# A fused attention and expert kernel: how the first batch's weights are signalled, loaded and split

## What is computed

```python
xn = _layernorm(x, axis=-1)
x = x + attention(xn, Wq, bq, Wk, bk, Wv, bv, Wo, bo) + experts(xn, ...)

# attention, 16 heads of 16
q, k = elu(xn @ Wq + bq) + 1, elu(xn @ Wk + bk) + 1
v = xn @ Wv + bv
kv = einsum('bkhd,bkhm->bhdm', k, v)
out = einsum('bqhd,bhdm->bqhm', q, kv)
out = out / maximum(einsum('bqhd,bkhd->bqh', q, k), 1e-6)[..., None]
return out @ Wo + bo

# experts: a shared swiglu, and the two best of four experts in the better of two groups
shared = swiglu(flat @ w_in.T) @ w_out.T
h = swiglu(flat @ w1.T)
routed = sum over e of (h * w_se[:, e:e + 1]) @ w2[e].T
return shared + routed
```

## Time and profile before

| | us |
|---|---|
| median of 3 runs | 922.63 (922.33 to 922.94) |
| the profiled execution | 922.05 |
| its span in the trace | 920.2 |
| TensorE busy | 903.5 (98%) |
| VectorE, ScalarE, GpSimd busy | 694.1, 367.3, 403.9 |
| mean granted TensorE clock | 0.996 |

### The profile page before, as it was taken

The page is one execution under the profiler, slowest core; times in us unless marked ns, Lnnn a source line. Parts: engine busy times, 40 slices in busy tenths (PEclk is TensorE's granted clock), DMA queues, the critical chain, the costliest instruction groups (busy, mean ns, idle before and its releaser), DMA issues. The chain is left out here.

```text
span 920.2 us, 22781 instructions
## 1 busy us (share of the span) xinstructions
PE 903.5 (98%) x6982; PEld 815.6 (89%) x6983; DVE 694.1 (75%) x1816; ACT 367.3 (40%) x605; POOL 403.9 (44%) x486
## 2 busy tenths in 40 slices
PE   8999999999999999999999999999999999999996
PEld 7798988889898989888898989898888999999996
DVE  6878777787868687777878696877676777777773
ACT  5654544353545445443525454453432222222220
POOL 3654342443425243424434243434242666555554
PEclk9999999999999999999999999999999999999999
DMA  6432413132322324141323223241156888888870
GB/s 216 136 116 70 125 51 120 69 103 90 93 100 93 116 69 125 46 125 69 103 80 103 91 92 126 69 125 47 59 204 144 145 143 143 148 137 135 137 128 1
DMA packets 141992, 98.63 MB, mean 107 GB/s; under 512 B 53136, under 2 KB 133008, under 8 KB 141968
## 3 DMA queue, kind: packets, MB, share of 16 engines
q1 hardware_dynamic: 103584, 62.50, 23.7%
q0 software_dynamic: 15920, 25.32, 12.5%
q10 hardware_dynamic: 22464, 10.51, 4.8%
HBM read 53.29 MB, written 46.43 MB: 108 GB/s over the span
## 5 line engine op out<-in xcount | busy, mean ns | idle before, releaser
L350 PE MATMUL bank<-wexp_hi,xnT_hi 128*128 (+1 forms) x560 | 188.1, 336 | 1.5 <-DVE xnT_lo L1149 1.1
L352 PE MATMUL bank<-wexp_hi,xnT_lo 128*128 (+1 forms) x560 | 185.7, 332 | 0.0
L351 PE MATMUL bank<-wexp_lo,xnT_hi 128*128 (+1 forms) x560 | 185.7, 332 | 0.0
L1227 POOL TENSOR_TENSOR h_lo<-gated,h_hi 128x256 fp32r<-128x256 f32 x128 | 98.7, 792 | 141.2 <-ACT h_hi L709 141.2
L350 PEld LDWEIGHTS bank<-wexp_hi,xnT_hi 128*128 128x128 f32 x560 | 106.3, 190 | 15.1 <-issue 4.6
L352 PEld LDWEIGHTS bank<-wexp_hi,xnT_lo 128*128 128x128 f32 x560 | 106.4, 190 | 10.3
L351 PEld LDWEIGHTS bank<-wexp_lo,xnT_hi 128*128 128x128 f32 x560 | 106.4, 190 | 9.5
L350 PE MATMUL bank<-xnT_hi,win_hi 128*128 128x512 f32 x256 | 102.1, 399 | 0.0
L351 PE MATMUL bank<-xnT_lo,win_hi 128*128 128x512 f32 x256 | 100.4, 392 | 0.0
L352 PE MATMUL bank<-xnT_hi,win_lo 128*128 128x512 f32 x256 | 99.6, 389 | 0.0
L1251 POOL TENSOR_TENSOR res<-res,bo_t 128x256 f32<-128x256 f32 x64 | 49.2, 801 | 112.3 <-DMA res<-x 112.3
(11 more groups left out here) (198 smaller groups left out, 2377.4 us busy)
## 6 DMA issues: line engine op xcount, KB each, us to landing
res<-x SPq DMA_DIRECT2D x16, 512.0 KB, 3.6
out<-res SPq DMA_DIRECT2D x16, 512.0 KB, 2.8
xt<-x SPq DMA_DIRECT2D x15, 512.0 KB, 3.4
xn_d<-xt SPq DMA_DIRECT2D x15, 512.0 KB, 4.9
xt<-xn_d SPq DMA_DIRECT2D x60, 128.0 KB, 2.7
xt<-h_d SPq DMA_DIRECT2D x76, 64.0 KB
xt<-h_d ACTq DMA_DIRECT2D x76, 64.0 KB
kb<-h_d SPq DMA_DIRECT2D x76, 64.0 KB
```

The lines of the kernel that those rows point to most:

```text
L350: e.matmul(to, w_hi, m_hi_, start=first_, stop=False, skip_group_check=free)
L351: e.matmul(to, w_hi, m_lo_, start=False, stop=False, skip_group_check=free)
L352: return e.matmul(to, w_lo, m_hi_, start=False, stop=last_, skip_group_check=free)
L1227: ins = pool.tensor_tensor(h_lo[:, j, cols], gated[:, j % 2, cols], h_hi[:, j, cols].bitcast(f32), ALU.subtract)
```

## The change

`kv_w_ld` becomes three semaphores, and ScalarE waits for each just ahead of its high part. `w_split` counts one more step, because W_k and router are split apart. The identity is loaded by itself; the rest of `stay`, and all loads of SP behind it, are issued after a wait for W_k, with the rest of `stay` behind W_q and the biases. VectorE makes W_k's low part ahead of the normalise, and W_v's ahead of the transposed x's. The five copies of constants move from ahead of the batch to after the statistics of batch 1, and the waits for them (`const_set`) move back on ScalarE and TensorE. On ScalarE the high part of w1's second half moves ahead of the exponential of the logits; on GpSimd the root of batch 1 moves behind the low part of w1's second half.

```diff
--- before.py
+++ after.py
@@ -187,14 +187,18 @@
         bank = [ctx.enter_context(nc.psum_tensor(f"bank{i}", [P, 512], f32)) for i in range(8)]
 
 
-        kv_w_ld = sem("kv_w_ld")
+        k_w_ld = sem("k_w_ld")
+        rt_w_ld = sem("rt_w_ld")
+        v_w_ld = sem("v_w_ld")
         q_w_ld = sem("q_w_ld")
         in_w_ld = sem("in_w_ld")
         out_w_ld = sem("out_w_ld")
         w1_ld = [sem(f"w1_ld{n}") for n in range(2)]
         x_ld = sem("x_ld")
         x0_ld = [sem(f"x0_ld{t}") for t in range(TB)]
+        ident_ld = sem("ident_ld")
         stay_ld = sem("stay_ld")
+        b_ld = sem("b_ld")
         c_ld = sem("c_ld")
         warm_set = sem("warm_set")
         r_ld = sem("r_ld")
@@ -365,10 +369,12 @@
             def loads(done, pairs, stage):
                 for to, of in [(buf, of) for buf, of, _, _ in stage] + pairs:
                     sp.dma_start(to, of).then_inc(done, 16)
-            loads(kv_w_ld, [], stage_kv[0:1])
-            sp.dma_start(stay[:, :], c_stay).then_inc(stay_ld, 16)
+            loads(k_w_ld, [], stage_kv[0:1])
+            sp.dma_start(ident, c_stay[:, 0:P]).then_inc(ident_ld, 16)
+            sp.wait_ge(k_w_ld, 16)
             loads(q_w_ld, [], stage_q)
-            loads(c_ld, [(bkl[:, :], b_kl), (bq[:, :], b_q)], [])
+            loads(b_ld, [(bkl[:, :], b_kl), (bq[:, :], b_q)], [])
+            sp.dma_start(stay[:, P:], c_stay[:, P:]).then_inc(stay_ld, 16)
             loads(in_w_ld, [], stage_in)
             loads(c_ld, [(round_f, c_round)], [])
             sp.wait_ge(xn_rdy, TB)
@@ -454,7 +460,7 @@
         def _(pe):
             def first_transposes():
 
-                pe.wait_ge(stay_ld, 16)
+                pe.wait_ge(ident_ld, 16)
                 for t in range(TB):
                     pe.wait_ge(xn_rdy, t + 1)
                     for c in range(DC):
@@ -501,7 +507,7 @@
                                  wk_hi[:, c, 0:KL], wk_lo[:, c, 0:KL], c == 0, c == DC - 1)
                     mm.then_inc(k_done, 1)
                     if first_row(b) and t == 0:
-                        pe.wait_ge(w_split, 2)
+                        pe.wait_ge(w_split, 3)
                     if t == 2:
                         pe.wait_ge(kb_rdy, TB * b + 1)
                     for c in range(DC):
@@ -511,7 +517,7 @@
                         mm.then_inc(v_done, 1)
 
                 if first_row(b):
-                    pe.wait_ge(w_split, 3)
+                    pe.wait_ge(w_split, 4)
                 for o in range(DC):
                     if o == 1:
                         wait(pe, base_rdy, DC * b - 1)
@@ -521,7 +527,6 @@
                     mm.then_inc(q_done, 1)
                 if first_row(b):
                     pe.wait_ge(ffn_split, 1)
-                    pe.wait_ge(const_set, 1)
                 wait(pe, base_rdy, DC * b)
                 pe.wait_ge(v_rdy, 2 * b + 1)
                 hidden(0, (6, 7))
@@ -545,6 +550,8 @@
                 pe.wait_ge(eq_rdy, DC * (b + 1))
                 routed(0, (3, 4))
 
+                if first_row(b):
+                    pe.wait_ge(const_set, 1)
                 pe.wait_ge(oh_rdy, b + 1)
                 W = NSLOT
                 pe.matmul(bank[5][:, 256:256 + TB * W], triones[:, 0, :], oh[:, :, :].rearrange("p t c -> p (t c)"),
@@ -629,7 +636,7 @@
 
             warm_up(WARM)
             first_transposes()
-            pe.wait_ge(w_split, 1)
+            pe.wait_ge(w_split, 2)
             rounds(pe, batch, B)
 
 
@@ -714,8 +721,7 @@
 
             def batch(b, last):
                 if first_row(b):
-                    act.wait_ge(w_split, 3)
-                    act.wait_ge(const_set, 1)
+                    act.wait_ge(w_split, 4)
                 for i in range(2):
                     act.wait_ge(v_done, 2 * b + i + 1)
                     wait(act, acc_done, b)
@@ -731,11 +737,13 @@
                     if first_row(b) and i == 0:
                         act.wait_ge(w1_ld[0], 16)
                         high_parts(stage_w1[0:1])
+                if first_row(b):
+                    act.wait_ge(w1_ld[1], 16)
+                    high_parts(stage_w1[1:2])
                 act.wait_ge(lg_rdy, b + 1)
                 act.activation(ex[:, :, :], lg[:, :, :], ACT.Exp).then_inc(ex_rdy, 1)
                 if first_row(b):
-                    act.wait_ge(w1_ld[1], 16)
-                    high_parts(stage_w1[1:2])
+                    act.wait_ge(const_set, 1)
                 for o in range(DC):
                     act.wait_ge(q_done, DC * b + o + 1)
                     act.wait_ge(phik_rdy, 2 * b + o + 1)
@@ -774,10 +782,11 @@
 
             for t in (1, 3):
                 act.dma_start(xt[:, t, :], x[0, t * P:(t + 1) * P, :]).then_inc(x0_ld[t], 16)
-            for buf, of, _, _ in stage_kv[1:3]:
-                act.dma_start(buf, of).then_inc(kv_w_ld, 16)
-            act.wait_ge(kv_w_ld, 16 * 3)
-            high_parts(stage_kv)
+            for (buf, of, _, _), done in zip(stage_kv[1:3], (rt_w_ld, v_w_ld)):
+                act.dma_start(buf, of).then_inc(done, 16)
+            for n, done in enumerate((k_w_ld, rt_w_ld, v_w_ld)):
+                act.wait_ge(done, 16)
+                high_parts(stage_kv[n:n + 1])
             first_high()
             act.wait_ge(q_w_ld, 16)
             high_parts(stage_q)
@@ -975,6 +984,16 @@
                 dve.wait_ge(rsil_rdy, TB * b + t + 1)
                 dve.tensor_tensor(hs[t], hs[t], bank[up_bank][:, :], ALU.mult).then_inc(rg_rdy, 1)
 
+            def constants_in():
+                dve.wait_ge(c_ld, 16)
+                dve.wait_ge(stay_ld, 16)
+                dve.tensor_scalar(nbq[:, :], bq[:, :], -1.0, None, ALU.mult)
+                dve.tensor_copy(triones[:, 0, :], tri_f)
+                dve.tensor_copy(spread[:, :, :], spread_f)
+                dve.tensor_copy(run[:, :], slot_row)
+                dve.tensor_copy(tok[:, :], tok0).then_inc(const_set, 1)
+                dve.wait_ge(const_set, 1)
+
             def batch(b, last):
                 start(LN_LINKS + PER * b)
 
@@ -999,6 +1018,7 @@
                     k_in(t)
                     if first_row(b) and t == 2:
                         stats_in(1)
+                        constants_in()
                     if first_row(b) and t == 3:
                         norm_out(1, True)
                     if t == 1 and not first_row(b) and not last:
@@ -1153,21 +1173,14 @@
             dve.memset(kvT[:, :, :], 0.0)
             start(0)
             norm(0)
+            low_parts(stage_kv[0:1], 0)
             first_normalise()
-            low_parts(stage_kv[0:2], 0)
+            low_parts(stage_kv[1:2], 1)
+            low_parts(stage_kv[2:3], 2)
             first_low()
-            low_parts(stage_kv[2:3], 2)
             low_parts(stage_q, len(stage_kv))
-            dve.wait_ge(c_ld, 16 * 3)
-            dve.wait_ge(kv_w_ld, 16 * 3)
-            dve.wait_ge(stay_ld, 16)
-            dve.tensor_scalar(nbq[:, :], bq[:, :], -1.0, None, ALU.mult)
-            dve.tensor_copy(triones[:, 0, :], tri_f)
-            dve.tensor_copy(spread[:, :, :], spread_f)
-            dve.tensor_copy(run[:, :], slot_row)
-            dve.tensor_copy(tok[:, :], tok0).then_inc(const_set, 1)
-            dve.wait_ge(const_set, 1)
-            dve.wait_ge(w_split, 3)
+            dve.wait_ge(b_ld, 16 * 2)
+            dve.wait_ge(w_split, 4)
             rounds(dve, batch, B)
 
             def add(t, g, n, to):
@@ -1300,8 +1313,7 @@
             for n in range(2):
                 pool.wait_ge(w_round, first + len(stage_in) + n + 1)
                 low_part(stage_w1[n][0], stage_w1[n][2], stage_w1[n][3], w1_split)
-                if n == 0:
-                    reciprocal_root(1)
+            reciprocal_root(1)
             in_low(2)
             in_low(3)
             pool.wait_ge(w_round, first + len(stage_in) + len(stage_w1) + 1)
```

## The result

The changed kernel took 924.85 us in the median (922.59 to 925.96), the kernel before 922.42 (920.65 to 923.66) on the same chips. The ratio is 1.0025 (95% interval 1.0018 to 1.0032): slower by 2.3 us (2.4 between the medians), just over the 0.2% that can be told from no change. The forecast was 922.1, a difference too small to be told. The profiled execution of after took 924.81 us, its span 923.0, 2.8 us over the span of before.

What follows compares the result with a forecast made beforehand. TensorE, busy 98% of the span, was taken as the bound, so only an earlier L588, its last first-batch wait, would count. Terms summed to -0.5 us there: 922.05 to 921.55, median 0.58 above, 922.1; range 920.7 to 923.3.

Steps and rivals of the forecast that it cites:

- The SP queue: Loads held behind the wait for W_k: W_in's landing unchanged, likely within -0.6 to +1.0 us; x at 14.2 us.
- sum for a clock that stays up: VectorE's K bias of row block 3 if TensorE's clock stays up: x last, 14.3 + 1.4 + 1.4 = 17.1 us, -1.0.
- The copies: Constants' copies on VectorE between batch 1's statistics and row block 3's K bias: cost 1.4 us, bounds 0.67 to 2.3.
- The first K matmul: TensorE's start: earlier W_k rounding and identity bring the first K matmul to 9.86 us from 10.61, -0.75.
- The moved root: GpSimd's root moved behind w1's low parts: contention costs VectorE +0.5 us at phiq, between -0.3 and +1.5.
- GpSimd's chain: GpSimd's low parts up to W_in: two gaps lost, 0.9 us, so the end at 28.3 plus any W_in delay.
- ScalarE behind phiq: ScalarE's early w1 cast frees it before gate(0) ends: -0.7 us between phiq and gate(1), gate(1) -0.5 in all.
- TensorE still gets there first: At L588 TensorE, 0.2 us later, still arrives before qn_hi, having waited 1.2 us, so L588 moves by -0.5.
- The sum: All terms together: phiq +0.2 us, L588 -0.5, profiled execution 921.55, median 922.1.
- Both signs: Prediction wrong if phiq starts before 28.7 or after 30.2 us, or TensorE waits between 14 and 27 us.
- Rival B: The load queue's hole makes W_in 2.5 us late: phiq +1.5, L588 +0.8, 923.4 us; chance 0.12.

Runs made afterwards that it cites:

- d1: The changed kernel repeated without any edit, against the kernel before: +1.7 us, ratio 1.0018 (1.0009 to 1.0026).
- a1: The changed kernel without SyncE's wait for W_k: +0.9 us against the kernel before, ratio 1.0010 (1.0001 to 1.0018).
- b3: The kernel before with only the five copies of constants moved behind batch 1's statistics: +0.8 us, ratio 1.0008 (0.9999 to 1.0017).
- c1: a6 with the copies of constants ahead of batch 1's statistics and the root back between w1's low parts: +0.4 us against before, ratio 1.0002.
- e1: c1 with the copies of constants at their old place, ahead of the first K bias: -0.8 us against before, ratio 0.9994 (0.9985 to 1.0003).
- a3: The changed kernel with GpSimd's root of batch 1 back between w1's two low parts: +2.0 us against before, ratio 1.0022 (1.0013 to 1.0031).
- b2: The kernel before with only GpSimd's root of batch 1 moved behind w1's second low part: +0.9 us, ratio 1.0007 (0.9998 to 1.0016).
- e2: The changed kernel with ScalarE's second w1 cast back behind the exponential: +2.9 us against before, ratio 1.0032 (1.0020 to 1.0045).
- a2: The changed kernel with the copies of constants ahead of batch 1's statistics: +2.6 us against before, ratio 1.0029 (1.0018 to 1.0040).
- a7: The changed kernel, SyncE's wait kept, with W_k's low part behind the normalise: +1.8 us against before, ratio 1.0017 (1.0008 to 1.0026).
- b4: The kernel before with only ScalarE's second w1 cast moved ahead of the exponential: -1.0 us, ratio 0.9989 (0.9981 to 0.9998).
- b1: The kernel before with only SyncE's wait for W_k added ahead of W_q's load: +1.5 us, ratio 1.0019 (1.0010 to 1.0028).
- a6: The changed kernel without SyncE's wait and with W_k's low part behind the normalise: +0.5 us against before, ratio 1.0006 (0.9997 to 1.0015).
- e3: b4 repeated without any edit, against the kernel before: -0.5 us, ratio 0.9995 (0.9986 to 1.0004).

## Why the prediction was wrong, step by step

**The SP queue: the step that failed.** I took W_in's landing as unchanged, "the bytes up to W_in's end are the same 2.7 MB", and x at 14.2. It landed at 17.0; W_in was 1.65 late, inside my bounds but beyond the value taken. The bytes were the same, but for 1.5 us nearly none moved, and nothing gave that back before 12 us. I had bounds for W_in only; for x, two loads further down the queue, I gave a value and no bound, and x was the one that VectorE waited for (2.14 us). By the prediction's own sum for a clock that stays up, 14.3 + 1.4 + 1.4 = 17.1, the last K bias came 3.3 late: 2.7 of that is x, 0.5 the copies. The "DMA: Bandwidth & Descriptors" page of the Trainium skill (Anatomy of one DMA), by whose fixed cost W_in would have been 1 to 2 us late, was the better guide here: W_in was 1.65 late in after and 2.2 in d1. The page gives that cost for DMAs issued by GpSimd, these were issued by SyncE, and x was 2.9 late.

**The copies (1.4 taken, bounds 0.67 to 2.3).** They measured 1.9 us in after, inside the bounds, and 1.2 in d1 and 2.4 in a1. How much they cost hangs on x: in b3, with x on time, the last K bias came at 17.63. c1 against e1 shows that a place ahead of the statistics costs too, 0.75 us at phiq in those traces.

**The first K matmul (-0.75).** It was -0.30. The working was right and said where it was thin: W_k landed 0.6 later than in before, and each 0.1 past 5.25 went into the normalise, 0.42 in all.

**The moved root (+0.5 by contention).** This was the term I "weighed most", and the traces do not agree on it. From the last K bias to phiq VectorE took 10.97 us in after against 11.20 in before, and 11.90 in d1, the same kernel as after; with the root put back (a3) it took 11.48, and a3's median can't be told from the changed kernel's. In after the second phi_k (L1009) still ran in 0.68, and three short steps behind it took 0.59 to 0.69 in its stead. GpSimd's w1 part beside them took 3.38 us instead of 2.83, so the two engines do hold each other up. That agrees with the GPSIMD Engine Reference of the Trainium skill (Specifications); the section doesn't say which of the two pays. Where a price of the root can be seen, in b2 and e2, it lies on GpSimd's own chain.

**GpSimd's chain (28.3).** It ended at 30.97. It began 1.64 later. The first part of w1 then followed without its wait, and up to the second the lag was down to 0.18; I had counted that second wait (0.42) as gone, yet it was 0.89, since ScalarE's cast sat behind work that waited for VectorE's late last K bias. Then 0.55 for the slower part and 1.01 for the root, which had lain in a wait before: 0.18 + 0.55 + 1.01 = 1.74. So in after the late W_in had been caught up here, and it was the late K bias that held this chain; in a2 and a7, where that bias was early, GpSimd ran on without the wait.

**ScalarE behind phiq (-0.7).** From phiq to gate(1) it was 4.29 us and is 3.55, so -0.74; b4 shows the same alone. This was sized right, and it is the only part of the change with a gain in both its trace and its median.

**L588: "TensorE still gets there first".** It did not, in the first profile, because the clock fell behind phiq. The clock stayed up over the K and V phase, where I had left it open. That brought the K bias of row block 2 forward by 1.84 us, and VectorE then waited for x. I had not asked where the fall would go instead.

**The sum.** Predicted phiq +0.2 and L588 -0.5. Measured: phiq +2.33 (last K bias) - 0.23 = +2.10, gate(1) +2.10 - 0.74 = +1.36, then +0.26 on VectorE and +0.47 by the clock, L588 +2.09; then +0.7 at the stage boundary, and 922.05 + 2.8 is the 924.8 of the profiled execution. Both signs that I had named for being wrong are there: phiq behind 30.2, and a wait of TensorE (2.7 us, to 24.68) between 14 and 27. The sum is that of one execution: in d1, the same kernel, 0.8 us of it is missing at L595. Rival B was the right mechanism with the wrong victim: it had W_in's chain 2.5 late and +0.8 at L588, and left out x. I gave B 0.12 because "late issue need not be late landing"; the landing times of b1, of after and of d1 all say otherwise.

**What stays open.** Why the rate stays at 117 to 262 GB/s from 8 to 11.5 us, once the queue is running again. Why some kernels lose another 0.5 to 1 us at the start of the weight-gather stage, 650 us behind the edit: it varied from draw to draw, and no run here was made for it. What the 0.5 to 0.9 us are made of that a1 and a6 still lose is open as well: root and copies are candidates, but neither has an interval that leaves no change out. And a clean run of the wait alone is missing, one in which ScalarE's table load stays in its place.

## What to carry to other kernels

A wait on the queue that issues the loads is paid by loads far behind it, not by the first one: here about 0, 1.7, 2.9 and 2.9 us at W_q, W_in, x and w1. Follow every load of that queue to who uses it, and give each one that somebody waits for a bound. When work is moved, look for the idle time in which it stood: the root had been free, and cost its 1.0 us at the end of GpSimd's chain once it stood behind a wait, while the cast that moved into a wait brought L588 forward by 0.7. Where two chains meet within 0.1 us, an edit to one of them is soon met by the other; of a1, a2, a3 and a7 only a1, which takes out the cause that both share, has a lower median (+0.9, the others +1.8 to +2.6). And when one edit is tested alone, compare the whole start with the kernel before: in b1 something else had moved.

## What the runs showed of the hardware

- In after, a queue held by a wait for one landing left a hole of 1.5 us below 60 GB/s, and the rate stayed above 300 GB/s only from 4.5 us later on.
- The same 256 KB load, third in its queue, landed after 3.2 to 5.2 us.
- VectorE and GpSimd hold each other up in either direction: the same w1 part took 2.82 to 3.38 us on GpSimd, and VectorE's gsum<-ex took 0.15 us in every trace in which GpSimd waited or ran the root beside it, and 0.69 or 0.70 in every trace in which GpSimd was in a w1 part.
- ScalarE's table load of 1.28 us ran at 2.6 us in sixteen traces, and in b1 at 7.45, behind the landing for which ScalarE waited.
- TensorE's granted clock fell once in the first batch in most profiled executions, at about 10.5 to 13 us in the kernel before and those near it, at about 24 to 34 us in the changed kernel and those near it; in b3, c1, e1, e2 and e3 it did not fall there. Where it fell mattered more than whether. In after, a1, a2, a6 and a7 it fell after 32 us, and L588's product started 1.20 to 2.74 us behind the start of qn_hi, in all others 0.74 or 0.75. In the K phase a fall shows nothing at phiq: b4 and e3 are the same kernel, with a fall at 11 us and with none, and phiq came at 29.09 and 28.91.
